# Biases of q, k and the first feed-forward layer added by ScalarE instead of TensorE, and low parts of q and k in the causal batches made by POOL from SBUF

## What is computed

```
x = x + masked attention(layernorm(x), ctx)                       one head, 256 wide
x = x + mixture of 4 transformer encoder layers, 2 picked per sequence:
        q,k,v = xn @ Win.T + bin ; 16 heads of 16 ; softmax ; out projection ; layernorm
        relu(x1 @ W1.T + b1) @ W2.T + b2 ; layernorm ; weighted by the gate
x = x + causal 16-head attention: q from layernorm(x), k and v from ctx, biases bq, bk, bv, bo
x = x + gated feed-forward (shared part for all tokens, one of 8 experts for 512 tokens)
```

## Time and profile before

| | |
|---|---|
| median of 3 runs | 840.95 us |
| profiled execution | 838.61 us, span 836.8 us |
| PE busy | 730.0 us (87% of the span) |
| VectorE (DVE) busy | 650.5 us (78%) |
| ScalarE (ACT) busy | 337.1 us (40%) |
| POOL busy | 378.6 us (45%) |
| granted TensorE clock, mean | 0.93 of full |

### The profile page before, as it was taken

The page is one execution under the profiler, slowest core; times in us unless marked ns, Lnnn a source line. Parts: engine busy times, 40 slices in busy tenths (PEclk is TensorE's granted clock), DMA queues, the critical chain, the costliest instruction groups (busy, mean ns, idle before and its releaser), DMA issues.

```text
span 836.8 us, 29143 instructions
## 1 busy us (share of the span) xinstructions
PE 730.0 (87%) x10976; PEld 580.5 (69%) x10976; DVE 650.5 (78%) x1858; ACT 337.1 (40%) x710; POOL 378.6 (45%) x647
## 2 busy tenths in 40 slices
PE   6978569999999999999999999998889888734895
PEld 5767547888888888888888888875556656412673
DVE  4686555878878797787878788879999999845865
ACT  4665324343443434344343444344445445411200
POOL 1788613344453544445353454542354445245132
PEclk9996579999999999999999999999999999955797
DMA  7677400000000000000000000002322222122000
GB/s 270 221 223 243 158 1 3 3 3 4 2 3 2 3 3 4 3 2 4 3 3 4 3 4 9 9 22 64 99 78 70 77 90 72 39 81 79 6 1 6
DMA packets 24651, 41.22 MB, mean 49 GB/s; under 512 B 3725, under 2 KB 16663, under 8 KB 24265
## 3 DMA queue, kind: packets, MB, share of 16 engines
q1 hardware_dynamic: 23096, 37.39, 13.7%
q0 software_dynamic: 704, 1.71, 0.7%
q10 hardware_dynamic: 722, 0.28, 0.1%
HBM read 30.85 MB, written 8.91 MB: 48 GB/s over the span
## 4 chain that ended last, share of the span: by engine, by line
PE 66%; DVE 16%; POOL 7%; issue 7%; ACT 3%; DMA 1%; POOLq 0%; ACTq 0%; DVEq 0%; SPq 0%
PE ps L475 7%; PE ps L469 7%; PE ps L477 6%; PE ps L476 6%; PE ps L670 6%; PE ps L652 5%; DVE mx L1389 5%; PE ps L602 4%; PE ps L708 3%; POOL w_lo L1812 3%; PE ps L710 3%; PE ps L709 3%; PE ps L604 3%; PE ps L603 3%; PE ps L594 2%
## 5 line engine op out<-in xcount | busy, mean ns | idle before, releaser
L1026 ACT ACTIVATE pT<-ps 128x1024 f32<-128x1024 f32 x96 | 93.1, 1021 | 126.1 <-PE ps L652 126.1
L1785 POOL TENSOR_TENSOR rs<-mv,cst 128x1 f32<-128x1 f32 x132 | 31.0, 235 | 179.7 <-DVE mv L1160 142.0
L1389 DVE TENSOR_REDUCE mx<-ps 128x16 f32<-128x2048 f32 x48 | 109.5, 2281 | 1.0 <-PE ps L625 1.0
L1873 POOL TENSOR_TENSOR y<-y,vec 128x256 f32<-128x256 f32 x32 | 23.2, 724 | 171.0 <-DVE y L1163 171.0
L708 PE MATMUL ps<-xh,w_hi 128*128 128x128 bf16 x512 | 99.4, 219 | 0.1
L709 PE MATMUL ps<-xl,w_hi 128*128 128x128 bf16 x512 | 99.3, 219 | 0.0
L710 PE MATMUL ps<-xh,w_lo 128*128 128x128 bf16 x512 | 99.2, 219 | 0.0
L1787 POOL TENSOR_TENSOR rs<-rs,cst 128x1 f32<-128x1 f32 x132 | 73.0, 553 | 10.3
L475 PE MATMUL ps<-w_hi,hh 128*128 x256 | 69.8, 273 | 0.0
L477 PE MATMUL ps<-w_lo,hh 128*128 x256 | 69.8, 273 | 0.0
L476 PE MATMUL ps<-w_hi,hl 128*128 x256 | 69.8, 273 | 0.0
(11 more groups left out here) (364 smaller groups left out, 2510.9 us busy)
## 6 DMA issues: line engine op xcount, KB each, us to landing
stage<-in_w SPq DMA_DIRECT2D x32, 384.0 KB, 3.7
vec<-in_vec SPq DMA_DIRECT2D x4, 896.0 KB, 5.9
vec<-in_tw SPq DMA_DIRECT2D x12, 256.0 KB, 2.7
ctxc<-in_ctx SPq DMA_DIRECT2D x19, 128.0 KB, 2.3
comb<-x SPq DMA_DIRECT2D x16, 128.0 KB, 1.7
comb<-t SPq DMA_DIRECT2D x16, 128.0 KB, 1.8
shared<-x1b SPq DMA_DIRECT2D x16, 128.0 KB, 1.7
out<-x SPq DMA_DIRECT2D x16, 128.0 KB, 1.8
```

Source lines behind the costliest of these rows:

```text
L1026: A(pT[:, 8 * a:8 * a + 8, :].rearrange("p h q -> p (h q)"), ps[:, 2 * a:2 * a + 2, :].rearrange("p g k -> p (g k)"), ACT.Exp, scale=SCALE ...
L1389: nc.vector.tensor_reduce(mx[:, :], att.rearrange("p g s k -> p (g s) k"), AX.X, ALU.max, negate=True).then_inc(m_max, 1)
```

## The change

The bias rows become per-partition columns: `bcol` holds, for each encoder layer and for the causal attention, 8 columns for the hidden layer and 4 for q and k. Their products on TensorE are gone. ScalarE reads each 128-column block of PSUM with its bias column as the activation's bias. In the encoder units it writes q, k (`qf`, `kf`) and relu (`hf`, or a part of `h`) in fp32 to SBUF, then rounds from SBUF; VectorE makes the low parts from the SBUF copies. In the causal batches ScalarE makes `qh` and `khm` from PSUM in six operations, later the fp32 copies `qf` and `kfm` in six more, and POOL subtracts. Several waits follow the new copies (`qk_sb`, `hr_a`, `hr_b`). The rows to SBUF at the start and their rounding are gone too; `ids`, `gidx`, `sidx` and `dsm` move into `ones`, to make room.

```diff
@@ PE: projection_qk (hidden likewise, 8 products)
-                    mm(dst, b1hl[:, B_QK + 128 * j:B_QK + 128 * j + 128], row_of(e), start=True, stop=False)
-                        mm(dst, w1, ycT_hi[:, src, :], start=False, stop=False)
+                        mm(dst, w1, ycT_hi[:, src, :], start=(c == 0), stop=False)
@@ PE: second, block, block_c
                 if half == 1:
                     pe.wait_ge(hl_b, u + 1)
+                    pe.wait_ge(hr_a, u + 1)
+                else:
                     pe.wait_ge(hl_a, u + 1)
-                    pe.wait_ge(hl_b, m - 2)
+                    pe.wait_ge(hr_b, m - 2)
-                    pe.wait_ge(qk_split, m + 1)
+                    pe.wait_ge(qk_sb, m + 1)
                     prep(kp, isinstance(kp, int) and kp >= B)
@@ ACT
+            def qk_full(u):
+                act.wait_ge(qk_psum, u + 1)
+                if u > 0:
+                    act.wait_ge(qk_split, u)
+                for j in range(2 * KC):
+                    dst = (qf if j < KC else kf)[:, j % KC, :]
+                    last = A(dst, ps[:, 4, 128 * j:128 * j + 128], ACT.Identity, bias=bias_of(u, B_QK + j))
+                last.then_inc(qk_sb, 1)
             def qk_hi(u):
+                act.wait_ge(qk_sb, u + 1)
+                copy(qh[:, :, :], qf[:, :, :])
+                for s in range(2):
+                    last = A(khm[:, :, s, :], kf[:, :, :], ACT.Copy, scale=mask_eo[s])
+                last.then_inc(qkT_hi, 1)
+            def qk_hi_causal(u):
                 act.wait_ge(qk_psum, u + 1)
+                for c in range(KC):
+                    A(qh[:, c, :], ps[:, 4, 128 * c:128 * c + 128], ACT.Identity, bias=bias_of(u, B_QK + c))
                 for s in range(2):
+                    for c in range(KC):
+                        last = A(khm[:, c, s, :], ps[:, 4, D + 128 * c:D + 128 * c + 128], ACT.Identity,
+                                 bias=kmb[:, 2 * s + c:2 * s + c + 1], scale=mask_eo[s])
                 last.then_inc(qkT_hi, 1)
+            def qk_full_causal(u):
+                act.wait_ge(qk_split, u)
+                ... (as qk_hi_causal, fp32 into qf and kfm)
+                last.then_inc(qk_sb, 1)
             def relu(u, half):
                 act.wait_ge(h_b if half else h_a, u + 1)
-                A(hh[:, 4 * half:4 * half + 4, :], ps[:, 7 - half, :].rearrange("p (c k) -> p c k", k=128),
-                  ACT.Relu).then_inc(hh_b if half else hh_a, 1)
+                if u > 0:
+                    act.wait_ge(hl_b if half else hl_a, u)
+                for j in range(FC // 2):
+                    last = A(hfs[half][:, j, :], ps[:, 7 - half, 128 * j:128 * j + 128], ACT.Relu,
+                             bias=bias_of(u, FC // 2 * half + j))
+                last.then_inc(hr_b if half else hr_a, 1)
+                act.wait_ge(hr_b if half else hr_a, u + 1)
+                copy(hh[:, 4 * half:4 * half + 4, :], hfs[half]).then_inc(hh_b if half else hh_a, 1)
@@ ACT: block
+                if attends(n):
+                    oo(n)
                 if encodes(f):
                     relu(f, 1)
-                if attends(n):
-                    oo(n)
                 shift(m)
                 if encodes(f):
                     relu(f, 0)
+                if n < UNITS:
+                    qk_full(n + 2)
@@ ACT: block_c
                 if served(b + 1):
-                    qk_hi(m)
+                    qk_hi_causal(m)
                 if served(b):
                     o_evict(n)
+                if served(b + 1):
+                    qk_full_causal(m)
                 if served(b - 1):
                     sh_y(b - 1)
@@ DVE
             def qk_low(u):
                 dve.wait_ge(qkT_hi, u + 1)
-                tt(ql[:, :, :], ps[:, 4, 0:D].rearrange("p (c k) -> p c k", k=128), qh[:, :, :], ALU.subtract)
+                dve.wait_ge(qk_sb, u + 1)
+                tt(ql[:, :, :], qf[:, :, :], qh[:, :, :], ALU.subtract)
                 for s in range(2):
-                    last = stt(klm[:, :, s, :], kk, mask_eo[s], khm[:, :, s, :], ALU.mult, ALU.subtract)
+                    last = stt(klm[:, :, s, :], kf[:, :, :], mask_eo[s], khm[:, :, s, :], ALU.mult, ALU.subtract)
             def h_low(u, half):
+                tt(hl[:, 4 * half:4 * half + 4, :], hfs[half], hh[:, 4 * half:4 * half + 4, :],
+                   ALU.subtract).then_inc(hl_b if half else hl_a, 1)
@@ DVE: block_c
                     bias_v(m, 1 - slot, vc[:, VC_V:VC_V + D])
-                    qk_low(m)
@@ POOL
+            def qk_low_causal(u):
+                pool.wait_ge(qkT_hi, u + 1)
+                pool.wait_ge(qk_sb, u + 1)
+                tt(ql[:, :, :], qf[:, :, :], qh[:, :, :], ALU.subtract)
+                tt(klm[:, :, :, :], kfm, khm[:, :, :, :], ALU.subtract).then_inc(qk_split, 1)
@@ POOL: block_c
                     x_bias(b + 1, 1 - slot)
+                    qk_low_causal(b + UNITS + 1)
                 if served(b - 4):
                     sh_sum(b - 4)
```

More of the change, by code:

```diff
@@ L72 @@
 C_ALL = C_POW + WORD
[L74 to L78, removed]
+K_SEL, K_CS, K_CT, K_ALL = 0, 512, 640, 768
+B_QK, B_EXP = FC, FC + 2 * KC
+B_ALL = (E + 1) * B_EXP
 def batch_of(u):
@@ L753, in block @@
                 if not isinstance(m, int) or m > 2:
-                    pe.wait_ge(hl_b, m - 2)
-                projection_v(None if causal_m else ex(1)[0])
+                    pe.wait_ge(hr_b, m - 2)
+                projection_v(None if causal_m else ex(1))
                 if encodes(g):
-                    second(g, 1, ex(-2)[0])
+                    second(g, 1, ex(-2))
                 if attends(n):
@@ L764, in block @@
                 if encodes(g):
-                    second(g, 0, ex(-2)[0])
+                    second(g, 0, ex(-2))
                 if fetch is not None:
@@ L778, in block @@
                 if encodes(f):
-                    hidden(f, 0, *ex(-1))
+                    hidden(f, 0, ex(-1))
                 shift_transpose(m)
                 if attends(n):
-                    out_proj(n, None if causal_n else ex(0)[0])
+                    out_proj(n, None if causal_n else ex(0))
                 if next_k is not None:
-                    pe.wait_ge(qk_split, m + 1)
-                    base, e = (None, E) if causal(n + 2) else ex(2)
-                    projection_qk(next_k, base, e)
+                    pe.wait_ge(qk_sb, m + 1)
+                    projection_qk(next_k, None if causal(n + 2) else ex(2))
                 scores_T(m, causal_m)
@@ L794, in block_c @@
                 if more:
-                    projection_qk(b + (B + 1), None, E)
+                    projection_qk(b + (B + 1), None)
                 if served(b):
@@ L856, in _ @@
             for b in range(1, B + 4):
-                block_c(b, b % 2, ex_of(UNITS - 1)[0] if b == 1 else None)
+                block_c(b, b % 2, ex_of(UNITS - 1) if b == 1 else None)
             pe.wait_ge(tw_lo, TCHUNKS)
@@ L985, in _ @@
                     copy(kst[:, :], kraw).then_inc(cst_ready, 1)
-                if i == 2:
-                    act.wait_ge(b1_zero, 1)
-                    act.wait_ge(b1_in, 16 * 4)
-                    for c0, width, rows_f in b1f:
-                        last = copy(b1hl[0:NROW, c0:c0 + width], rows_f)
-                    last.then_inc(b1_hi, 1)
             act.wait_ge(yT_psum, 1)
@@ L1108, in block_c @@
                     sh_e(b - 1)
+            act.wait_ge(b1_in, 16)
+            act.wait_ge(g_words, 1)
+            words_act = [word_of(act, 0)]
+            qk_full(0)
             for n in range(-1, UNITS + 1):
+                if n % WORD == WORD - 4 and n // WORD + 1 < UNITS // WORD:
+                    words_act.append(word_of(act, n // WORD + 1))
                 block(n, prep_of(n + 2))
+            act.wait_ge(vones_ready, 6)
+            act.wait_ge(hl_a, UNITS)
             for b in range(1, B + 4):
@@ L1281, in _ @@
                         nc.vector.memset(v2[slot][:, :, HD:HD + 1], 1.0).then_inc(vones_ready, 1)
+                    dve.wait_ge(b1_in, 16)
+                    for s in range(2):
+                        ts(kmb[:, 2 * s:2 * s + 2], bcol[:, E * B_EXP + B_QK + KC:B_ALL], mask_eo[s], None,
+                           ALU.mult).then_inc(vones_ready, 1)
             stats(x[:, 0:D], 0, 0, y_stats, y_var)
@@ L2000, in _consts @@
     k[:, K_CT:K_CT + 128] = np.where(p[:, None] > p[None, :], -1e30, 0)
-    for e in range(NROW):
-        k[[e, 32 + e], K_ROW + e] = 1
     return c, k, np.arange(M, dtype=np.float32)[None, :]
```

71 lines of the change are left out of this document (31 added, 40 removed).

## The result

The changed kernel takes 866.16 us (median of 4 runs, 865.62 to 870.23) against 840.27 us (4 runs) of the kernel before on the same chip: ratio 1.034, 95% interval 1.031 to 1.037. Slower, as forecast (861 us, range 845 to 882). The profiled span grew from 836.8 to 864.3 us, by 27.5; the sum of the prediction had 20.4 for it.

A forecast was written before the change was run, and what follows sets the result against it. VectorE's maximum was taken to set the time, TensorE's products filling its gap. Sum: 838.6 - 1.0 + 1.3 + 4.8 + 14 + 1.3 = 859.0, plus 2.3 for the median: 861 us, range 845 to 882.

The forecast's parts named there:

- TensorE is not the bound; the products give back nothing: Hidden layer's eight products per encoder unit counted 0, q and k's four -0.1 us; rival, TensorE the bound: 815 us, chance 0.12.
- ScalarE's prices: A 128-column ScalarE operation is spaced 0.25 us with one column operand, 0.36 with two; rival, second column free: 847 to 849, 0.13.
- Causal batches, +14 from `xh`: ScalarE's added operations make `xh` and `xl` later, +1.0 us per batch in 14 batches; ends +0.1 and +2.1 per batch.
- TensorE's wait for `mtile`: In a causal batch, a sign of the forecast: this wait near 2.7 us instead of 1.49.
- Causal batches, +1.3 from a collision: VectorE's line 1547 meets POOL's `ql`: 0.1 us in 13 batches; rival, `klm` first and encoder colliding twice: 881 us, 0.13.
- The clock: A fall of the granted clock in the causal batches was named as a sign that the prediction is wrong; no term.
- Encoder units, +4.8: `hl` collides with POOL in every second unit: +0.4 - 0.1 us per pair, times 16; without collision -3.2, with twice +11.
- ScalarE's relu, put at +0.1 us for each `hl`: In encoder units, relu becomes four operations and a cast: +0.1 us for the first `hl`, +0.1 for the second.
- The gain of 0.1 in every second unit for q and k: In encoder units without the POOL collision, the four q and k products taken out give back 0.1 us.
- Start of unit 0, +1.3: Nothing hides `qk_full` before unit 0: 3 x 0.25 + 0.37 and its address, +1.3 us.
- Stage of pairs, -1.0: VectorE loses four subtractions on bias rows, ScalarE four casts, beside arriving weights: between 0 and -3.4 us, taken -1.0.

The follow-up runs named there:

- no_products: The kernel before, with the twelve bias products of an encoder unit left out on TensorE and nothing put in their place: 838.1 us, 0.999.
- one_column: The changed kernel, with the scale column taken off the eight masked k operations of a causal batch, leaving the bias column: 865.3 us, 1.032.
- late_low: The changed kernel, with POOL's last sum and tw first in causal batches and its low parts of q and k behind mtile: 859.7 us, 1.025.
- both_orders: The changed kernel with POOL's order of late_low, and ScalarE's xh and w_hi ahead of the six fp32 copies: 850.6 us, 1.014.
- encoder_te: The changed kernel with all biases of the encoder units on TensorE as before, only the causal batches as changed: 857.1 us, 1.023.
- hl_psum: The changed kernel, with VectorE's hl in the encoder units made from PSUM again, ScalarE's and TensorE's work kept: 862.8 us, 1.028.
- hidden_te: The changed kernel with the encoder's hidden layer as before (bias products on TensorE, hl from PSUM), q and k as changed: 860.0 us, 1.024.
- all_orders: The changed kernel with both_orders' ScalarE order, POOL's low parts, sum and tw behind mtile, xl ahead of o_rs, earlier word load: 852.0 us, 1.016.
- xh_first: The changed kernel, with the copy of xh ahead of the six fp32 copies in ScalarE's program of a causal batch: 865.8 us, 1.031.

## Why the prediction was right, and where its steps were not

- **TensorE is not the bound; the products give back nothing.** Right, shown by no_products. The reason given for the hidden layer was half of it: TensorE hardly arrives earlier. Line 700 starts every 0.23 us there (410.62, 410.85) though only three products of 0.06 us stand in that time; the register instructions for the addresses are the likely pace, which no run tested. From the end of `xl` to the transpose of the shifts it took 4.29 us before (399.10 to 403.39) and 4.13 now (406.90 to 411.03), though eight products of 0.06 us went.
- **ScalarE's prices.** 0.25 with one column: right (2 in 0.49). With two 0.36: measured 0.34 (652.52 to 653.89, four). The second column costs 0.09 to 0.10. The Trainium skill, "ScalarE: Activation LUTs", section "What ACT_TABLE_LOAD costs", says about 93 ns for each; one_column agrees. By that price the prediction named 12.9 us for the causal term; with both groups of copies counted it is about 12, an estimate from the page's figure.
- **Causal batches, +14 from `xh`.** The mechanism was right and is shown by late_low, both_orders and encoder_te; `xh` cost 0.90 a batch and not 1.0, in 13 batches, 11.7 us. The fourteenth lies in the transition and shows none of it: encoder_te has 43.1 us there, before 43.3. TensorE's wait for `mtile` was put near 2.7 and is 1.88: its products on `xl` stand ahead of that wait and moved along.
- **Causal batches, +1.3 from a collision.** Right that POOL and VectorE would meet, wrong about where in all batches but one. Line 1582 (1547 before) took 0.32 or 0.33 us in twelve of 13, and 0.76 in the first. POOL's added work pushed its old sum and `tw` from under the maximum to its end, into the rounding of `mtile`: 0.43 a batch. With the first batch that makes 5.2 us, four times the term. In the last two batches the same shift took something away: before, line 1547 met `tw` there and took 1.00 us (one of them is the earlier trace rows), which is why they took 12.77. The prediction had followed POOL's two new operations and not those queued behind them. The prediction looked only at an operation with two operands in SBUF; the rounding has one. By the Trainium skill, "SBUF — State Buffer", section "Who interferes with whom", copies, casts and tensor_scalar can take the shared ports too, where their operands allow it; the 0.63 us of the cast and the 1.29 us of `y` agree.
- **The clock.** Not in the sum: one batch at 0.89, +1.6 us. The prediction had named a fall in the batches as a sign that it is wrong, and in this it was; the sum left it out. With late_low's shorter wait it did not come in the profile. Together transition and batches grew by 18.1 us, forecast 15.3; a steady batch grew by 1.33, forecast 1.0 to 1.1.
- **Encoder units, +4.8.** Measured 8.1. The collision came as forecast, and where; taking it away gives back 3.0 us (hl_psum), where the prediction had 6.4 against 1.6 gained. The mis-sized step is ScalarE's relu, put at +0.1 us for each `hl`. The first `hl` starts 0.48 behind the end of `ool` and started 0.23 behind it; the second ends 0.31 late with no collision (hl_psum). The hidden layer as before gives back another 3.7 us (hl_psum against hidden_te); since that run also puts back TensorE's eight products and ScalarE's old order, the 3.7 are the relu's at most. The 0.9 of the transition come on top and were in no term. The gain of 0.1 in every second unit for q and k did not show as time.
- **Start of unit 0, +1.3.** Measured 2.25. The copies take 1.5 of it; 0.8 is ScalarE's load of the packed word, which stood behind a wait for the causal weights and was not priced. all_orders gets that part back. The row of the first copy:

```profile
105.59 0.62 ACT L1006 ACTIVATE qf<-ps,bcol 128x128 f32<-128x128 f32 x2 [7.69 <-POOL stage L1865]
```

- **Stage of pairs, -1.0.** The gate's words come 0.1 us earlier in this pair of profiles; by the scatter of 2 us nothing can be said of it.

The forecast was right in sign and cause. In the span it came 7.1 us low: too little for POOL and VectorE meeting (3.9), the encoder (3.3), the clock (1.6), the start (0.9), the transition (0.9) and the stage of pairs (0.9), too much for `xh` (2.3) and for the last two batches, which lost their old meeting (1.3); the rest fell by 0.8. That it is not further off is in part luck, since the 4.4 us too much hide a part of the 11.5 too little. In the medians it was 5 us low. One thing stays open: why a TensorE wait of 1.87 or 1.88 us lowers the clock in one batch of thirteen in the changed kernel and in every second of one_column. The length of the wait alone does not decide it: in xh_first ten waits are 2.71 us long, and the clock fell behind three of them; before the change one is 2.12 us long (at 712.94), and the batch behind it kept its full clock.

## What to carry to other kernels

An engine at 40% busy may still have no slack at the one place where others wait: price added work by what stands behind it in its engine's program, down to the last operation before the next wait, on each engine that gets some. When a loss has two causes in a row, taking away one may show nothing (xh_first): repair them together before calling either harmless. Work taken off a full engine is worth only the distance to the next wait, here nothing that could be measured.

## What was not expected of the hardware

- TensorE's granted clock fell behind waits of 1.88 us in a stretch busy at 77% (10.40 of 13.47 us), and one fall cost 1.6 us. hl_psum, hidden_te and encoder_te, with the same waits, have one such batch each (15.06 to 15.09 us); with waits of 1.70 us (no_products), 1.49 (before), 1.40 (late_low) and 1.15 (both_orders) no steady batch of the profiles has one.
- VectorE operations with a single tensor in SBUF (the cast of 64 columns, 0.20 us alone and 0.63; the normalization of 256, 0.41 alone and 1.29) end 0.05 and 0.15 us behind the POOL operation at their side.
- ScalarE read 256 columns no faster from SBUF than from PSUM: `khm` takes 541 ns on average from SBUF and took 498 from PSUM.

```profile
L1013 ACT ACTIVATE khm<-kf,cst 128x256 bf16<-128x256 f32 x68 | 32.1, 541 | 0.0
```
